# Self-attention of a decoder layer: float16 parts for the weighted values, and one fixed turn per group of heads

## The reference

```python
def _L0_attn_ref(x, w_q, w_k, w_v, w_o):     # x is layer-normalised, H = 16, DK = DV = 64, C = 256
    q = jnp.einsum('ntc,hdc->nhtd', x, w_q)
    k = jnp.einsum('ntc,hdc->nhtd', x, w_k)
    v = jnp.einsum('ntc,hdc->nhtd', x, w_v)
    a = jnp.einsum('nhtd,nhsd->nhts', q, k) / jnp.sqrt(jnp.asarray(dk, x.dtype))
    a = jnp.where(mask[None, None], jnp.asarray(-jnp.inf, a.dtype), a)
    a = jax.nn.softmax(a, axis=-1)
    y = jnp.einsum('nhts,nhsd->nthd', a, v)
    return y.reshape(...) @ w_o
```

## Time and profile before

| | |
|---|---|
| median of 3 runs | 2292.13 us (2290.48 to 2292.91) |
| the profiled execution | 2309.25 us, its span 2307.5 us |
| self-attention in the span | from 0 to about 1011 us |
| share of busy time over the span | PE 86%, DVE 61%, ACT 52%, POOL 30% |
| mean granted TensorE clock | 0.931 of 2.4 GHz |

### The profile page before, as it was taken

The page is one execution under the profiler, slowest core; times in us unless marked ns, Lnnn a source line. Parts: engine busy times, 40 slices in busy tenths (PEclk is TensorE's granted clock), DMA queues, the critical chain, the costliest instruction groups (busy, mean ns, idle before and its releaser), DMA issues. The chain is left out here.

```text
span 2307.5 us, 37967 instructions
## 1 busy us (share of the span) xinstructions
PE 1978.6 (86%) x13464; PEld 1002.5 (43%) x13464; DVE 1403.0 (61%) x3126; ACT 1193.6 (52%) x2157; POOL 702.0 (30%) x693
## 2 busy tenths in 40 slices
PE   4899999999999999967999999983988898679972
PEld 2556565655565556542233222321333333246641
DVE  5664656564656565526778676765478876544344
ACT  2554545454545454534777666771456664335531
POOL 2110201110111110122333223303457765532266
PEclk8999999999999999987899888995899999799997
DMA  5111111111111011113122232201001110133355
GB/s 155 46 38 38 38 38 37 37 38 38 37 28 44 22 40 36 37 50 58 42 49 55 51 56 56 47 1 45 1 10 42 60 53 22 46 94 124 105 160 155
DMA packets 97081, 122.82 MB, mean 53 GB/s; under 512 B 14304, under 2 KB 73984, under 8 KB 96896
## 3 DMA queue, kind: packets, MB, share of 16 engines
q1 hardware_dynamic: 79872, 93.11, 17.1%
q0 software_dynamic: 6144, 16.79, 2.3%
q10 hardware_dynamic: 10880, 10.49, 1.4%
HBM read 52.64 MB, written 33.82 MB: 37 GB/s over the span
## 5 line engine op out<-in xcount | busy, mean ns | idle before, releaser
L1104 DVE TENSOR_REDUCE x_NM<-x_pm 128x1 f32<-128x512 f32 x512 | 343.5, 688 | 127.2 <-PE x_pm L847 125.1
L1029 ACT ACTIVATE x_PR<-x_pS 128x512 f32<-128x512 f32 x512 | 300.9, 601 | 136.4 <-PE x_pS L863 130.8
L376 PE MATMUL a_pa<-a_PR,a_V 128*128 128x512 f32 (+3 forms) x1024 | 341.8, 441 | 0.7 <-ACT a_PR L456 0.3
L456 ACT ACTIVATE a_PR<-a_pS 128x384 f32<-128x384 f32 (+1 forms) x384 | 201.4, 525 | 207.2 <-PE a_pS L365 204.9
L538 DVE CUSTOM_DVE_ANT_0 a_pm<-a_pm,a_causal 128x128 f32<-128x128 f32 (+3 forms) x512 | 247.2, 509 | 83.8 <-PE a_pm L351 69.0
L611 POOL CAST a_YT_hi<-a_Y 128x512 f16<-128x512 f32 x64 | 40.2, 628 | 760.3 <-DVE a_Y L546 760.3
L847 PE MATMUL x_pm<-x_KT,x_QT 48*128 48x512 f16 x512 | 208.9, 427 | 23.0 <-DMA x_QT<-q_k_parts 22.3
L863 PE MATMUL x_pS<-x_QT,x_KT 49*128 49x512 f16 x512 | 204.4, 416 | 15.4 <-ACT x_PR L1029 14.3
L546 DVE TENSOR_TENSOR a_Y<-a_pa,a_RS 64x512 f32<-64x512 f32 x128 | 88.0, 688 | 182.4 <-ACT a_RS L464 181.3
L376 PEld LDWEIGHTS a_pa<-a_PR,a_V 128*128 128x128 f32 x1024 | 174.8, 192 | 29.7 <-ACT a_PR L456 11.3
L351 PE MATMUL a_pm<-a_KA,a_QA 128*128 128x128 f16 (+3 forms) x512 | 142.5, 308 | 43.7 <-DVE a_NM L538 27.9
(11 more groups left out here) (361 smaller groups left out, 4506.2 us busy)
## 6 DMA issues: line engine op xcount, KB each, us to landing
a_QA<-a_nat_q SPq DMA_DIRECT2D x128, 128.0 KB, 2.3
m_xr<-sent SPq DMA_DIRECT2D x80, 128.0 KB
made<-e_eo ACTq DMA_DIRECT2D x40, 256.0 KB
a_KA<-a_nat_k SPq DMA_DIRECT2D x64, 128.0 KB, 2.3
a_KB<-a_nat_k SPq DMA_DIRECT2D x64, 128.0 KB, 2.4
x_KT<-q_k_parts SPq DMA_DIRECT2D x48, 128.0 KB, 4.3
x_QT<-q_k_parts SPq DMA_DIRECT2D x48, 128.0 KB, 4.3
m_xr<-in_w SPq DMA_DIRECT2D x12, 512.0 KB
```

Of the source, the lines that this page charges most:

```text
L376: m = eng.matmul(pa[j % 2][:, P * kc:T], V[:, u % 2, kc, j, :], PR[:, i % 4, at:at + T - P * kc], start=(kc == 0), stop=(kc == TT - 1))
L456: eng.activation(PR[:, i % 4, 0:n], pS[i % 2][:, 0:n], ACT.Exp, scale=SCALE).then_inc(s_e, 1)
L1029: eng.activation(PR[:, kc, j, :], pS[i % 2][:, :], ACT.Exp, scale=SCALE).then_inc(s_e, 1)
L1104: eng.tensor_reduce(NM[:, v % 2, c:c + 1], ring_bank("max", v, n)[:, :], AX.X, ALU.max, negate=True).then_inc(s_red, 1)
```

## The change

Four things change, all in self-attention.

First, the weighted values go from one float32 matmul to three float16 matmuls per block (`V_hi` by `P_hi`, `V_lo` by `P_hi`, `V_hi` by `P_lo`). ACT takes the exponential of each slot twice, to float32 `PR` and to float16 `P_hi` (E and H); POOL subtracts them to `P_lo` (LO, 12 per unit); DVE makes `V_lo` with four instructions per unit. The maxima get a bias so that the exponentials reach up to 256 and their low parts stay in float16's range. A slot of scores is free after H instead of E, and a slot's weighted values wait for LO instead of E.

Second, the low parts of queries and keys go to `nat` whole (4 DVE instructions per unit instead of 8), and SP copies them too: 12 DMAs per unit instead of 8, in three groups with a semaphore each (queries, keys, keys for `KB`). `QA` and `QB` have three buffers.

Third, the order is no longer a loop but a table `PLACE` of positions in a turn of 27.0, one list per engine and step; each engine's threads are merged by these keys. The keys set the order alone, nothing waits for a time. Scores and weighted values of a unit are spread over the two turns after its projections. On SP the rows of maxima are a thread of their own beside the placing of queries and keys. The reciprocal's exponential runs on both heads of a pair at once (2 per unit instead of 4). The output is projected one block of 128 rows per turn (24 matmuls in two halves, bank `pp0` alone), five turns behind.

Fourth, at the start the weights have two staging buffers instead of four, and POOL's presets stand ahead of the first normalisation.

```diff
-    V = sb("V", [P, 2, TT, GH, P], F32)
+    RQ = 3
+    nat = [[sb(f"nat_{n}_{m}", [P, 2, T], F16) for n in ("q", "k")] for m in ("hi", "lo")]
+    QA, QB = (sb(n, [P, RQ, 2, 2, T], F16) for n in ("QA", "QB"))
+    V = [sb(f"V_{n}", [P, 2, TT, GH, P], F16) for n in ("hi", "lo")]
...
+    TURN = 27.0
+    PLACE = {
+        ("PE", "QK"): (0, 3.181, 9.46, 15.912),
...
+        ("SP", "CQ"): (15.95,),
+        ("SP", "CK"): (18.79,),
+        ("SP", "CKB"): (19.676,),
+        ("SP", "NP"): (44.562,),
+    }
+    def at(engine, step, u, i=0):
+        return u * TURN + PLACE[engine, step][i]
...
-            eng.wait_ge(s_e, US * u + i + 1)
+                eng.wait_ge(s_el, US * u + i + 1)
...
+                for kc, a in SLOTS[sl]:
+                    for n, (v, p) in enumerate(((0, 0), (1, 0), (0, 1))):
+                        m = eng.matmul(pa[j % 2][:, P * kc:T], V[v][:, u % 2, kc, j, :], P16[p][:, i % RH, a:a + T - P * kc],
+                                       start=(kc == 0 and n == 0), stop=(kc == TT - 1 and n == 2))
...
+                eng.activation(PR[:, m % RF, 0:n], pS[i % 2][:, 0:n], ACT.Exp, scale=SCALE).then_inc(s_e, 1)
+                yield at("ACT", "H", u, i)
+                after(eng, s_av, m + 1 - RH)
+                eng.activation(P16[0][:, m % RH, 0:n], pS[i % 2][:, 0:n], ACT.Exp, scale=SCALE).then_inc(s_eh, 1)
...
+        def exp_low(u):
+            for i in range(US):
+                yield at("POOL", "LO", u, i)
+                m, n = US * u + i, slot_width(i % NS)
+                eng.wait_ge(s_e, m + 1)
+                eng.wait_ge(s_eh, m + 1)
+                after(eng, s_av, m + 1 - RH)
+                eng.tensor_tensor(P16[1][:, m % RH, 0:n], PR[:, m % RF, 0:n], P16[0][:, m % RH, 0:n],
+                                  ALU.subtract).then_inc(s_el, 1)
...
+        side_by_side(over(rows_of_maxima), over(copies), load_weights())
```

More of the change, by code:

```diff
@@ L312, in project_qk, with over, transpose_x @@
+    def over(thread, n=NU):
+        for i in range(n):
+            yield from thread(i)
+    def tensor_program(eng):
+        def transpose_x(b, half):
+            eng.wait_ge((s_xhi, s_xlo)[half], b + 1)
+            if half == 0:
+                after(eng, s_vlo, 2 * NG * b)
+            else:
+                after(eng, s_xr, NG * b - 5)
+            turned(eng, pp[1 - half], xn16[half], k).then_inc(s_xt, 1)
         def project_qk(u, c):
             b, g = u // NG, u % NG
+            if u < NG and c == 0:
+                eng.wait_ge(weights.split_done, 2 * u + 1)
@@ L330, in project_v @@
             g = u % NG
+            if u < NG and h == 0:
+                eng.wait_ge(weights.split_done, 2 * u + 2)
             eng.wait_ge(s_lo, 4 * u + 3 + h)
@@ new lines, in projections @@
+        def projections(u):
+            b, g = u // NG, u % NG
+            if g == 0 and u < NU:
+                for h in range(2):
+                    yield at_turned("PE", b, h)
+                    transpose_x(b, h)
+            for c in range(4 if u < NU else 0):
+                yield at("PE", "QK", u, c)
+                project_qk(u, c)
+            for h in range(2 if u < NU else 0):
+                yield at("PE", "V", u, h)
+                project_v(u, h)
+            if u >= 5:
+                yield from project_out(u)
@@ L496, in vector_program, with split_weights @@
+        def split_weights():
+            for n in range(NW):
+                yield at_split(n)
+                weights.high(eng, n)
+        eng.preload_act_table_set("natural_log_exp_and_others")
+        side_by_side(over(reciprocals), over(exponentials), over(maxima_out), over(projections), over(x_high, B), split_weights())
     def vector_program(eng):
         def statistics(b):
+            if b < 2:
+                eng.wait_ge(s_x[b], 16)
             for t in range(TT):
@@ new lines, in reduce_max @@
+        def reduce_max(u):
+            for i in range(4 * GH):
+                yield at("DVE", "MX", u, i)
+                eng.wait_ge(s_mx, 16 * u + i + 1)
+                if i == 0:
+                    eng.wait_ge(s_causal, 1)
+                    after(eng, s_nt, u)
+                n = (i % TT + 1) * P
+                eng.tensor_tensor_reduce(out=pm[i % 2][:, 0:n], in0=pm[i % 2][:, 0:n], in1=causal[:, T - n:T], scale=1.0,
+                                         scalar=NEG, op0=ALU.add, op1=ALU.max, accum_out=NM[:, column(i)]).then_inc(s_red, 1)
@@ new lines, in scale_values, with split_weights @@
+        def scale_values(u):
+            for j in range(GH):
+                pair, q = j // 2, 2 * u + j // 2
+                yield at("DVE", "Y", u, j)
+                eng.wait_ge(s_rc, q + 1)
+                after(eng, s_yl, q - 1)
+                outs, _ = rows_of(j)
+                eng.tensor_tensor(Y[outs, pair, :], pa[j % 2][outs, :], RS[outs, pair, :], ALU.mult).then_inc(s_y, 1)
+        def split_weights():
+            for n in range(NW):
+                yield at_split(n) + 1.3
+                weights.low(eng, n)
```

524 lines of the change are left out of this document (236 added, 288 removed).

## The result

| | before | changed |
|---|---|---|
| median of 4 runs each | 2291.31 us | 2174.26 us |
| lowest run | 2277.97 us | 2165.57 us |
| the profiled execution | 2309.25 us | 2168.20 us, its span 2166.5 us |
| end of self-attention in the span | 1011.8 us | 892.1 us |

The ratio is 0.9489, with a 95% interval of 0.9427 to 0.9550: the changed kernel is faster by 117 us. The forecast was 2171, in a range of 2142 to 2235. (One of the four runs of the changed kernel, 2426 us, was disturbed: the median above contains it, without it the median is 2168 us, and the ratio leaves it out.)

The account below looks back on a forecast made before the run. PE bounds self-attention: 24.6 us of work plus 1.2 of waits make a turn of 25.8 us against 29.9, ending the stage 121 us earlier. From the median, 2292.13 - 121 = 2171 us, range 2142 to 2235.

Parts of the forecast that it names:

- the waits of the old order: PE's 3.2 us of waits per turn before: third projection on a low part, maxima on DVE reductions and behind eight copies.
- The currency: PE work counted from matmul start to start: 0.216 us per 512 float16 columns, 0.86 in float32; 23.9 us per unit before.
- the forecast's 24.6 us: PE's work per turn after the change: 23.9, minus 2.1 for weighted values, plus 2.6 output projection and 0.2 transposes.
- the slacks near zero at the first scores and values: First scores, waiting for maxima rows, and first values, waiting for LO, cost PE half a microsecond together per plain turn.
- restarting weight loads: Weight loads that a stopped PE has to start again add 0.2 us per turn.
- 2.0 us per batch to the normalisation: Statistics on DVE between reductions add 1.3 us, the second copy of transposed x 0.7; 0.5 us per turn.
- the walk: A turn laid out by hand, PE back to back and other engines behind their inputs, to find where PE would wait.
- The slacks on SP: SP's six query copies end at 11.4 in the turn, just as NM's rows arrive; first scores wait 0 to 0.2 us.
- the rival's price: SP's queue delays maxima and scores when a low part comes 2.5 us late: turn 28.3 us, 2244 us, chance 0.07.
- the slower rival: DVE and POOL get in each other's way, so DVE needs 32.3 us and sets the turn: 2360 us, chance 0.05.
- The start: POOL's presets first cost about nothing (-1 to +3 us); first NM at about 50, first two turns 26 us each.
- The end: After the last NM, ACT's pace and four output blocks on one bank add 3 us (0 to +8), making 41.

Follow-up runs that it names:

- e1: Changed kernel with the weighted values back to one float32 matmul per block, one exponential per slot and no low parts, in the new order: 2212.26 us, ratio 0.9651.
- e9: The changed kernel unaltered, run again as control beside e5, e6 and e7: 2155.06 us, ratio 0.9444 to the kernel before.
- e5: Changed kernel with the next batch's normalisation earlier: statistics and root by 23 of the table's 27, normalised x by 14: 2141.19 us, ratio 0.9367.
- e3: Changed kernel with SP's rows of maxima behind the unit's six key copies instead of ahead of them: 2405.66 us, ratio 1.0498.
- e6: Changed kernel with SP's weight loads 6 later in the turn and the last weight split 13 later: ratio 0.9436 to the kernel before.
- e7: Changed kernel with the edits of both e5 and e6: 2137.94 us, ratio 0.9355 to the kernel before.
- e4: Loop order of the kernel before with the new arithmetic alone, three float16 matmuls per block: 2391.76 us, ratio 1.0421.
- e8: Changed kernel with the third projection of a unit on PE right behind the second, as in the kernel before: ratio 0.9625.

## Why the prediction was right, step by step

The time and its two main mechanisms came out as forecast: PE's work sets the plain turn, and the waits of the old order are gone. The split of the gain, the size of the waits and the start did not.

**The currency.** Three float16 matmuls for each block, on PE's timeline of the changed kernel:

```profile
685.45 0.38 PE L463 MATMUL a_pa<-a_P_hi,a_V_hi 128*128 128x512 f16 x1
685.67 0.38 PE L463 MATMUL a_pa<-a_P_hi,a_V_lo 128*128 128x512 f16 x1
685.88 0.38 PE L463 MATMUL a_pa<-a_P_lo,a_V_hi 128*128 128x512 f16 x1
```

0.216 us apart, 0.65 for a block, as forecast from the earlier trace rows. The unit's work was right to 0.1: the forecast's 24.6 us hold 0.2 for transposes of x, of which a plain turn has none, and the plain turn took 24.46. The saving was 2.3 where the sum has 2.1: in e1 a float32 block of 512 columns, of which a unit has four, took 0.91 us (690.95 to 691.86), not 0.86.

**The two halves.** The total agrees to 2 us (119.7 and 121), its parts do not: by e1 the arithmetic brought 48 us of the stage where the forecast had 67, and the order 71.5 where it had 54. The errors cancel, so the nearness of the total says less of the theory than it seems to. What holds of the mechanism is the work of PE per turn, the waits that lost their cause, and that the order makes the room.

**The waits.** I charged half a microsecond to each plain turn for the slacks near zero at the first scores and values, and 0.2 for restarting weight loads. Both are zero: no row of a plain turn's PE shows idle time. This is the largest miss in the steady part. I charged 2.0 us per batch to the normalisation; the two turns it touches are 0.9 and 1.7 us longer than their work (25.4 and 27.0 against 24.5 and 25.3), 2.6 us. The largest waits of PE's weight loads in 500 to 800 us, and a row of PE's timeline:

```profile
PEld a_pm L428 <- issue: 5.6, 4, 2.6
PEld a_pm L432 <- DVE a_NM L604: 3.6, 3, 1.2
PEld a_pp L365 <- DVE a_xT_lo L560: 1.8, 3, 0.6
PEld a_pp L380 <- DVE a_nat_k_lo L582: 1.6, 3, 0.5
...
533.96 0.33 PE L428 MATMUL a_pm<-a_KA,a_QA 128*128 128x128 f16 x2 [2.17 <-issue]
```

NM behind the reductions that the statistics held up, and the projections behind the transposed x, are the two places named. The largest row is a third one that the forecast didn't charge: the first maximum, which stands behind four key copies and had a slack of 0.5 us in the walk. PE waits for it 0.6 us in a normalisation turn, and once 2.17 us, where one key copy held SP's queue for 1.65 us (528.69 to 530.34) instead of 0.63; why that copy was slow is not shown, and the same turn is as long in e9 (28.6 us in both). e5 took away the waits of NM and of the value projections and nearly all before the first maximum. It left that of the transposed x, 0.33 us on PE and 0.6 on its weight loads. In sum: 24.7 us of work with the transposes, 0.65 of waits around the normalisation, and 0.2 from irregular turns like that of 28.6 make the mean of 25.5, where the forecast had 24.6 and 1.2.

**The slacks on SP.** The forecast had SP free of the queries as NM's rows arrive, with the first scores in time. The changed kernel has no wait there in steady turns, and e3 shows what hangs on it: 6 us per turn, and up to 2 more by the clock, which the rival's price left out. That price, 28.3 us per turn, was for a delay of 2.5 us; it was not where the changed kernel stands.

**The other engines.** POOL 15.2 us in the plain turn (forecast 15.4), DVE 15.6 (about 16), ACT 17.9 (about 20). The last is too high since I added durations. Two rows of ACT's timeline:

```profile
688.00 0.49 ACT L508 ACTIVATE a_PR<-a_pS 128x384 f32<-128x384 f32 x1
688.38 0.48 ACT L511 ACTIVATE a_P_hi<-a_pS 128x384 f16<-128x384 f32 x1
```

The second starts 0.38 us behind the first, while each is listed with 0.49; 512 columns follow after 0.50 with 0.60. By starts the doubled exponentials add 4 x 0.50 + 8 x 0.38 = 5.0 us, and e1, without them, has 12.8 us on ACT where the changed kernel has 17.9. The rule that I used for PE, the time from start to start, holds for ACT as well.

**The contention.** DVE's low parts beside POOL's subtractions, and the subtractions themselves (min/median/max ns):

```profile
L645 POOL TENSOR_TENSOR a_P_lo<-a_PR,a_P_hi x384: 906/917/1299, 62.6 to 870.0; 128x384 f16<-128x384 f32 x128, 128x512 f16<-128x512 f32 x64
...
L582 DVE SCALAR_TENSOR_TENSOR a_nat_q_lo<-a_pp,a_nat_q_hi x64: 685/686/692, 24.8 to 824.1; 128x512 f16<-128x512 f32 x64
L582 DVE SCALAR_TENSOR_TENSOR a_nat_k_lo<-a_pp,a_nat_k_hi x64: 679/692/693, 29.5 to 830.8; 128x512 f16<-128x512 f32 x64
```

The 128 low parts on DVE spread over 14 ns, so the slower rival had no price here. Subtractions above the usual length are rare; one of 1.30 us, on the timeline of DVE and POOL:

```profile
107.31 1.32 DVE L121 SCALAR_TENSOR_TENSOR a_wo_lo<-a_w_stage,a_wo_hi 128x1024 f16<-128x1024 f32 x1 [2.88 <-ACT a_wo_hi L115]
...
108.11 1.30 POOL L645 TENSOR_TENSOR a_P_lo<-a_PR,a_P_hi 128x384 f16<-128x384 f32 x1 [0.55 <-ACT a_PR L508]
```

Beside it runs the weight split, whose two inputs both lie in SBUF. The Trainium skill (GPSIMD Engine Reference, Key points) states just this distinction between instructions that contend with GpSimd and those that do not; the trace agrees, with 1.30 us instead of 0.91 beside the split.

**The start: wrong, and hidden by other errors.** The first projection starts at 21.38 us, as before (21.36): the presets cost nothing, as forecast. The first NM comes at 53.4 (forecast 50), and the first two turns took 28.6 and 35.5 us where I had 26 each. By 117.5 us the kernel was 15 us behind the forecast. The other turns gave it back: the three to 191.9 brought 3 us, two of them being without output projection, 24 turns of 25.5 another 7, the next 1.4 and the last 4.4 (21.4 instead of 25.8). So the last NM came at 849.9, against 850: that this number was met to a tenth of a microsecond is luck. The step that failed is the one that counted the weights to split, 26 us for a turn, and not what their loads hold up on SP and their splits on DVE. From the timeline of the second of these turns:

```profile
82.29 0.27 ACT L500 ACTIVATE a_NMT<-a_pm 16x128 f16<-16x128 f32 x1
...
85.64 0.35 SPq L110 DMA_DIRECT2D a_w_stage<-in_a_wo  x1
86.03 1.40 SPq L706 DMA_DIRECT2D a_QB<-a_NMT  x2
...
89.56 0.59 PE L447 MATMUL a_pS<-a_QA,a_KA 128*128 128x512 f16 x1 [3.89 <-issue]
...
108.96 0.50 PE L428 MATMUL a_pm<-a_KA,a_QA 128*128 128x384 f16 x1 [2.88 <-DVE a_NM L604]
```

The rows of maxima are there at 82.6. SP issues them at 86.03, since a weight load stands ahead of them and waits for one of now only two staging buffers, which a weight split on DVE (83.97 to 85.61) had just set free. No run has the new order with four, so whether four would have spared it is not shown. PE stops for 3.9 us. In the turn before it stops for 5.3, of which e6 takes 2.5 away; 2.8 stay with the loads out of the way. Behind both stops the clock is at 0.50, in 90 to 95 us and in 60 to 64, as behind those of e3. The second stop of the second turn, 2.9 us at 108.96, has another cause: DVE's reductions stand behind the weight split at 107.31 (its row is shown above, under the contention), which waits 2.9 us for its high part on ACT. e6 removes the stop at the first scores of the second turn and that at 108.96, and brings its own of 5.3 us; it ends the stage 5.5 us earlier. e7's first two turns are still 25.5 and 31.1 us, so the weights cost something in both orders.

**The end.** From the last NM to the next stage 42.2 us, forecast 41, with 0.77 us between the output blocks where I had 0.9. The forecast left the clock out of it: PE stops for 4.7 us before the first of these blocks, and from 876.41 to 880.2 its matmuls of 256 columns start 0.213 us apart, with the granted clock at 0.50.

## What to carry to other kernels

An arithmetic that saves work on the bound engine and lengthens the chain to it is worth what the order makes of it: here plus 101 us in one order and minus 48 in another. Lay a turn out by hand, from start to start on every engine, and look at each slack near zero; then look at the fill apart, turn by turn, for blocking instructions of a queue (a load that waits for its buffer) ahead of the steady work. And judge a change of one stage by the end of that stage: the unchanged rest took from 1254 to 1302 us in the twelve profiled executions.

## What I had not expected of the hardware

A stop of PE can cost more than its length. In e3 a stop of 5.6 us was followed by 4 us at a granted clock of 0.50 with PE fully busy (834 to 838 us), which is 2 us lost; two neighbouring turns have 0.89 and 0.95 as their mean. In the changed kernel the stop of 3.9 us at its start was followed by 0.50 in 90 to 95 us, and the stops in its steady turns, the longest of them 2.2 us, left the clock at 1.00.

The unchanged rest of the program took 1295.7, 1274.4 and 1261.9 us in three profiled executions (before, changed, e9), with the same instructions and a mean clock of 0.89, 0.90 and 0.91; the extremes are e4 with 1301.9 at 0.88 and e8 with 1254.3 at 0.92.
